# A Trainium2 kernel of attention and soft experts: small layer-norm and output steps given other places in the hand-written order of the expert stage

## The chip, the cores and the metric

The kernel runs on one core of one Trainium2 chip. The metric is the device time of one execution in microseconds (us), as the median of several runs. A profiled execution gives a trace of the core's engines: PE is TensorE's matrix multiply, PEld its weight load, DVE is VectorE, ACT is ScalarE, POOL is GpSimd, and SP is the engine that issues most transfers. Each engine works through its own queue strictly in order and waits on semaphores that the others raise.

## The reference, cut to what matters

The input x has 2 sequences of 1024 rows with 256 columns. An attention layer with 16 query heads and 4 key and value heads is added to x and layer-normed; a soft mixture of 16 experts with 128 slots each is added to that and layer-normed again. The change lies in the second half:

```python
x = _layernorm(x + attn(x, Wq, Wk, Wv, Wo, head_scale))
...
mean = jnp.mean(x, axis=-1, keepdims=True)
var = jnp.mean(jnp.square(x - mean), axis=-1, keepdims=True)
x_ln = (x - mean) / jnp.sqrt(var + LN_EPS) * gamma + beta
x_n = _l2norm(x_ln, -1) * scale
logits = jnp.einsum('bnd,des->bnes', x_n, _l2norm(mu, 0))
dispatch = softmax(logits, axis=1)
combine = softmax(logits.reshape(B, N, E * S), axis=-1)
slot_in = jnp.einsum('bnd,bnes->besd', x_ln, dispatch)
h = gelu(jnp.einsum('besd,edh->besh', slot_in, W1) + b1)
slot_out = jnp.einsum('besh,ehd->besd', h, W2) + b2
out = jnp.einsum('bsd,bns->bnd', slot_out, combine)
x = _layernorm(x + out)
```

All of it is float32; products are made of two or three passes over a high and a low part.

## The kernel before, in words

The program has two stages, attention for both sequences and then the experts (`experts`). Both are written as a plan: a Python list of steps in one order, from which every engine takes, in that order, the steps that are its own. So the plan fixes the order in each queue, and the semaphores do the rest. `plan_experts` (line 987) writes the list of the expert stage; the change touches only that function.

The expert stage goes through 32 pairs of sequence and expert, 16 of sequence 0 and then 16 of sequence 1. A **step** is one turn of the loop over `s` at line 1079, 35 in all: in step s the pair s is turned and dispatched, and the logits of pair s + 1 are made. Four pairs are a **unit** (u is the unit of the step, j the place within it); the unit before, v, is spread over the rows in the meantime. What a step has, with lines:

- PE turns `exps` of the pair in two halves (`turn`, L1488). ACT copies the first half into `dispatch` (`turned_a`, L1617) and DVE the second (`turned_b`, L1831); below they are the two **turned copies**.
- PE makes the next pair's logits (L1478). DVE takes their maximum (`top`, L1812), ACT the exponential (L1683) and a copy of the logits (`keep`, L1694), and DVE a running maximum (`run`, L1825) and an inverse of the sum (L1848).
- In steps with odd j PE widens two inverses (`wide_inverse`, L1498; it needs the PSUM bank that the first turned copy frees), and gathers (L1527; it needs both turned copies).
- With j = 3 PE turns the running maximum (`peaks`, L1546; it needs the bank that the second turned copy frees), DVE reduces it (`peak`, L1902), PE widens it (`wide`, L1555), and ACT and DVE copy that (`widened_a`, L1716, and `widened_b`, L1917). GpSimd then subtracts it from the four kept logits of the unit (L2006).
- With j = 1 and 2 the weights of unit v are taken apart into a high part on ACT (L1728) and a low part, three on GpSimd (L1986) and the fourth on DVE (`weight_lo_b`, L1895).
- With j = 2 the **spread** of unit v over the first four row tiles runs on PE (L1577), 12 matmuls a tile, and DVE adds each to `ffn_mixed` (`combine`, L1923 or L1927); the other four tiles follow with j = 0. The spread's tenth matmul of the first tile needs `weight_lo_b`.

Beside these stand the steps of two layer norms, which the change gives other places:

- Sequence 1's rows are normed while sequence 0's pairs run. `stats` is a `bn_stats` and a `bn_aggr` on DVE for each of 8 tiles (L1750, L1752), at the ends of steps 2 and 6, four tiles each. Then `deviations` (vary, std_1, inv_1, std_2, inv_2, offsets) alternates nine small DVE operations with two square roots on ACT (L1623). `centre` is four ACT passes over two tiles (L1639, L1644), `gamma` and `beta` two on GpSimd (L1996), and `squares` two on ACT (L1661); with tile pairs 0 and 1 of `centre` after step 7, pairs 2 and 3 and the first two `squares` after step 10, and the other two after step 11.
- Sequence 0's output is finished while sequence 1's pairs run. `finish` adds the expert output to a row tile on DVE (L1933) and `stats_3` takes its moments (L1750, L1752); three tiles at the end of step 18, three of step 22, two of step 26. `vary_3`, `std_3` (a square root on ACT, L1628, with its activation table), `inv_3` (three small DVE operations, L1957 to L1961), eight `normal_a` on ACT (L1632) and two stores follow in steps 26 to 30.

For sequence 1 the same end comes in the last spread, which runs tile by tile (L1570).

The finish of a row tile, as the engines take it:

```python
put(("finish", b, t), ("stats_3", b, t))
finish(0, {experts + 2: (0, 1, 2), experts + 6: (3, 4, 5), experts + 10: (6, 7)}.get(s, ()))
```

## Time and profile before

| | |
|---|---|
| median of 3 runs | 1204.24 us (1203.88 to 1205.72) |
| the profiled execution's own time | 1204.42 us |
| its span, first to last instruction | 1202.6 us |
| mean granted TensorE clock | 0.986 of full speed |
| PE busy | 1139.5 us (95%) |
| DVE, ACT, POOL busy | 804.0, 791.9, 712.2 us (67, 66, 59%) |
| expert stage | from about 838 us to the end |

The span is 1.8 us shorter than the execution's own time, since it leaves out what lies ahead of the first and behind the last instruction. A busy share is a mean over the program: it tells which engine is nearest to its limit, not which wait is worth something. That is read from the stretch itself: from the timeline, where a row gives in brackets how long its engine stood idle before it and what released it, and from the windows, which give busy time and granted clock of a stretch.

### The profile page before, as it was taken

To read this page: it belongs to the slowest core of one execution; us is meant where nothing else is said; L and a number is where in the kernel's file an instruction comes from. 1 tells how busy PE (TensorE), PEld (TensorE's weight loads), DVE (VectorE), ACT (ScalarE), POOL (GpSimd) and SP (SyncE) were. 2 spreads that over 40 slices of the span, in tenths; PEclk is the share of its full clock that TensorE was granted. 3 is DMA by queue.
4 is the path that set the end of the run, shared out by engine and by line. 5 is a ranking of instruction groups with operands and counts; after the bars stand their busy time and mean duration, and the time that the engine had idled before them with its cause. 6 is when DMAs were issued, how large, how long until landed. Compare 5 with 4: busy or idle time off the path is not lost. (4 is left out here: it accounts for less than half of the span.)

```text
span 1202.6 us, 23558 instructions
## 1 busy us (share of the span) xinstructions
PE 1139.5 (95%) x8096; PEld 1048.5 (87%) x8096; DVE 804.0 (67%) x1899; ACT 791.9 (66%) x1654; POOL 712.2 (59%) x485
## 2 busy tenths in 40 slices
PE   5899999999999999999999999999999999999977
PEld 4799999999998998899999999998778888898866
DVE  4575676666677568667676766776676575777767
ACT  2566766666675666678776766664477795567654
POOL 2677667667774765678676675530276654565521
PEclk9899999999999999999999999999999999999989
DMA  3231121111211112111111111200101101010011
GB/s 101 71 123 45 36 53 45 32 28 50 58 28 32 45 32 58 39 37 28 49 37 48 32 45 36 49 7 19 36 23 27 28 18 32 19 28 19 10 44 36
DMA packets 48789, 47.57 MB, mean 40 GB/s; under 512 B 13080, under 2 KB 43288, under 8 KB 48416
## 3 DMA queue, kind: packets, MB, share of 16 engines
q1 hardware_dynamic: 48384, 45.99, 14.8%
q8 instruction: 67, 1.10, 0.4%
q14 instruction: 50, 0.41, 0.1%
q10 hardware_dynamic: 288, 0.07, 0.0%
HBM read 24.03 MB, written 2.10 MB: 22 GB/s over the span
## 5 line engine op out<-in xcount | busy, mean ns | idle before, releaser
L536 PE MATMUL ring<-kT,qT 128*128 128x384 f32 (+5 forms) x1152 | 244.2, 347 | 3.1 <-ACT exps L701 2.6
L701 ACT ACTIVATE exps<-ring,neg_max 128x128 f32<-128x128 f32 (+7 forms) x256 | 189.3, 742 | 55.9 <-DVE neg_max L845 55.0
L845 DVE CUSTOM_DVE_ANT_0 ring<-ring,hidden 128x128 f32<-128x128 f32 (+7 forms) x256 | 191.6, 769 | 22.0 <-PE ring L536 21.1
L718 ACT ACTIVATE exp_parts<-turned 128x512 fp32r<-128x512 f32 x192 | 114.6, 597 | 133.9 <-PE turned L551 113.6
L536 PEld LDWEIGHTS ring<-kT,qT 128*128 128x128 f32 x1152 | 186.0, 189 | 14.3 <-issue 3.7
L572 PE MATMUL mix<-exp_parts,v_parts 128*128 128x256 f32 x1152 | 184.5, 296 | 0.4 <-DVE exp_parts L863 0.4
L551 PE MATMUL turned<-ident,exps 128*128 128x128 f32 x1152 | 178.5, 273 | 4.5 <-DVE exp_parts L863 3.8
L551 PEld LDWEIGHTS turned<-ident,exps 128*128 128x128 f32 x1152 | 141.3, 141 | 22.8 <-issue 3.6
L863 DVE TENSOR_TENSOR exp_parts<-turned,exp_parts 128x512 fp32r<-128x512 f32 x192 | 131.9, 687 | 29.3 <-ACT exp_parts L718 29.1
L572 PEld LDWEIGHTS mix<-exp_parts,v_parts 128*128 128x128 f32 x1152 | 149.4, 190 | 0.6 <-DVE exp_parts L863 0.6
L973 POOL TENSOR_TENSOR cos_part<-taken,cos_sb 128x1024 f32<-128x1024 f32 x38 | 91.3, 2402 | 94.7 <-ACT taken L669 94.7
L857 DVE TENSOR_TENSOR diag_parts<-turned,diag_parts 128x256 fp32r<-128x256 f32 x128 | 54.0, 422 | 123.4 <-ACT diag_parts L711 123.4
L510 PE MATMUL ring<-xT,parts 128*128 128x512 f32 x528 | 132.8, 401 | 2.2 <-ACT exps L701 2.2
L976 POOL TENSOR_TENSOR rotated<-rotated,sin_sb 128x1024 f32<-128x1024 f32 x38 | 91.1, 2398 | 71.1 <-DMA rotated<-taken 71.1
L510 PEld LDWEIGHTS ring<-xT,parts 128*128 128x128 f32 x528 | 97.1, 190 | 21.7 <-issue 2.6
L584 PE MATMUL ring<-wo_sb,mixed 128*128 128x256 f32 x768 | 105.9, 287 | 1.2 <-DVE mixed L851 1.2
L878 DVE SCALAR_TENSOR_TENSOR y_sb<-ring,inv_sum,y_sb 128x256 f32<-128x256 f32 x256 | 105.7, 476 | 0.4 <-PE ring L584 0.3
L584 PEld LDWEIGHTS ring<-wo_sb,mixed 128*128 128x128 f32 x768 | 96.3, 191 | 1.9 <-DVE mixed L851 1.8
L980 POOL TENSOR_TENSOR cos_part<-cos_part,rotated 128x1024 f32<-128x1024 f32 x38 | 91.2, 2401 | 5.4
L851 DVE TENSOR_TENSOR mixed<-mix,mixed 128x256 fp32r<-128x256 f32 x128 | 53.6, 419 | 60.3 <-ACT mixed L725 57.7
L1577 PE MATMUL ffn_spread<-ffn_slots,ffn_weights 128*128 128x258 f32 x672 | 87.3, 288 | 5.0 <-DVE ffn_weights L1895 4.8
L1577 PEld LDWEIGHTS ffn_spread<-ffn_slots,ffn_weights 128*128 128x128 f32 x672 | 84.9, 193 | 7.2 <-DVE ffn_weights L1895 5.9
(225 smaller groups left out, 2185.1 us busy)
## 6 DMA issues: line engine op xcount, KB each, us to landing
rotated<-taken SPq DMA_DIRECT2D x76, 256.0 KB, 3.7
raw_q<-in_L_attn_Wq_dram SPq DMA_DIRECT2D x32, 128.0 KB, 3.6
raw_o<-in_L_attn_Wo_dram SPq DMA_DIRECT2D x32, 128.0 KB, 3.3
ffn_mu_next<-in_L_ffn_mu_dram SPq DMA_DIRECT2D x28, 128.0 KB, 2.4
y_sb<-in_L_attn_x_dram SPq DMA_DIRECT2D x2, 1024.0 KB, 7.4
exps_and_mu<-in_L_ffn_mu_dram SPq DMA_DIRECT2D x1, 2048.0 KB, 9.6
ffn_w_sb<-in_L_ffn_W_dram SPq DMA_DIRECT2D x8, 256.0 KB
ffn_w_sb<-in_L_ffn_W_dram SPq DMA_DIRECT2D x14, 128.0 KB, 2.6
```

Of the source, the lines that this page charges most:

```text
L510: last = nc.tensor.matmul(ring_cols(item, half * BANK, BANK), w[:, a, c, :], xT[b][:, m, c, half * BANK:(half + 1) * BANK], start=k == 0, ...
L536: last = nc.tensor.matmul(ring_cols(item, half * BANK, piece), qT[:, H % QUERIES, a, i * P:(i + 1) * P], kT[:, G % 2, m, half * piece:(hal ...
L551: last = nc.tensor.transpose(bank[:, k * P:(k + 1) * P], exp_row(w, i)[:, j * P:(j + 1) * P], ident[:, :])
L572: last = nc.tensor.matmul(mix[:, window % 2, 0:PAIR], v_parts[:, G % 2, a, j * P:(j + 1) * P], parts[:, m, half * PAIR:(half + 1) * PAIR], ...
L584: last = nc.tensor.matmul(ring_cols(item, t * D, D), mixed[:, window % 2, a, t * P:(t + 1) * P], wo_sb[:, H % 2, m, :], start=k == 0, stop ...
L701: nc.scalar.activation(dst, tile, ACT.Exp, bias=neg_max[:, H % 2, i:i + 1], scale=-1.0, accum_out=row_sum[:, H % 2, i:i + 1]).then_inc(don ...
L718: nc.scalar.activation(exp_parts[:, slot % HELD, 0, :], turned[:, n % 2, :], ACT.Copy).then_inc(done[kind], 1)
L845: nc.vector.tensor_tensor_reduce(tile, tile, later, -1.0, 3.0e38, ALU.add, ALU.min, neg_max[:, H % 2, i:i + 1]).then_inc(done[kind], 1)
L863: nc.vector.tensor_tensor(exp_parts[:, slot % HELD, 1, :], turned[:, n % 2, :], exp_parts[:, slot % HELD, 0, :].bitcast(F32), ALU.subtract ...
L878: last = nc.vector.scalar_tensor_tensor(y_row, ring_cols(("output", H, w), t * D, D), inv_sum[:, H % 2, i:i + 1], y_row, ALU.mult, ALU.add)
L973: nc.gpsimd.tensor_tensor(part, taken[:, :], cos_sb[:, :], ALU.mult).then_inc(done[kind], 1)
L1577: last = nc.tensor.matmul(spread_ps[:, t % 2, 0:WIDE], weights[:, a, k, t * P:(t + 1) * P], slots[:, m, k, :], start=k == 0 and n == 0, st ...
```

## The change

Only the plan's order changes; no instruction is added or removed but one load of an activation table on ACT (the square root `std_3` of sequence 0 no longer stands between exponentials). PE's and SP's orders are the same as before.

- Sequence 1's `stats`: three tiles behind the turned copies of step 2 and one at its end, two behind the `peak` of step 3, two behind the turned copies of step 6. `vary` and `std_1` move up to just behind the exponential and `keep` of step 6; the rest of `deviations` stays at the end of the step, ahead of the parts of mu and W1.
- `centre` of pair 2 moves to the middle of step 10, behind the weight's high part; `centre` of pair 3 and the first `squares` into step 11 ahead of the peaks; the other three `squares` to the end of step 11.
- Sequence 0's `finish`: one tile at the end of steps 18 and 22 (two at the end of 26, as before), one behind the peak of steps 19 and 23, one behind the turned copies of steps 22 and 26.
- `std_3` of sequence 0 moves to the end of step 33, `inv_3`, the eight normals and the two stores into step 34, between the second and the third tile of the last spread.

```diff
--- before.py
+++ after.py
@@ -1001,7 +1001,7 @@
         put(*[("stats", b, t) for t in ts])
 
     def deviations(b):
-        put(*[(kind, b) for kind in ("vary", "std_1", "inv_1", "std_2", "inv_2", "offsets")])
+        put(*[(kind, b) for kind in ("inv_1", "std_2", "inv_2", "offsets")])
 
     def output(v):
         put(("output", v, 0), ("output", v, 1))
@@ -1054,18 +1054,32 @@
         put(*[("unit_hi", b, j) for j in js])
         put(*[("unit_lo", b, j) for j in js])
 
+    def centre(j):
+        put(("centre", 1, j), ("gamma", 1, j), ("beta", 1, j))
+
+    def beside_turn(s):
+
+        if sequences > 1:
+            moments(1, {2: (0, 1, 2), 6: (6, 7)}.get(s, ()))
+            finish(0, {experts + 6: (2,), experts + 10: (5,)}.get(s, ()))
+
+    def beside_peak(s):
+
+        if sequences > 1:
+            moments(1, {3: (4, 5)}.get(s, ()))
+            finish(0, {experts + 3: (1,), experts + 7: (4,)}.get(s, ()))
+
     def early(s):
 
         if sequences == 1:
             return
-        if s in (2, 6):
-            moments(1, range(s - 2, s + 2))
-        if s == 6:
-            deviations(1)
-        for j in {7: (0, 1), 10: (2, 3)}.get(s, ()):
-            put(("centre", 1, j), ("gamma", 1, j), ("beta", 1, j))
-        for j in {10: (0, 1), 11: (2, 3)}.get(s, ()):
-            put(("squares", 1, j))
+        if s == 2:
+            moments(1, (3,))
+        if s == 7:
+            centre(0)
+            centre(1)
+        if s == 11:
+            put(*[("squares", 1, j) for j in (1, 2, 3)])
         if s == 12:
             put(("inv_length", 1))
         if s == 13:
@@ -1092,6 +1106,7 @@
         if live:
             for half in range(2):
                 put(("turn", s, half), ("turned_b" if half else "turned_a", s, half))
+            beside_turn(s)
         if ripe and j == 1 and not last_unit:
             if not unfolded:
                 slots(v, 1)
@@ -1101,10 +1116,10 @@
             put(("weight", v, 3))
         if ripe and j == 2 and not last_unit:
             weight_parts(v, 3)
+            if s == 10 and sequences > 1:
+                centre(2)
         if ripe and j == 0 and not changed and not last_unit:
             put(("gelu", v))
-        if s == experts + 12 and sequences > 1:
-            put(("std_3", 0, 0))
         if s == experts - 4 and sequences > 1:
             put(("length", 1))
         if ahead and not change:
@@ -1119,6 +1134,9 @@
             slots(v, 1)
         if j == 3:
             split_mu(s + 3)
+        if s == 11 and sequences > 1:
+            centre(3)
+            put(("squares", 1, 0))
         if s == experts - 2 and sequences > 1:
             turn_units(1, (0, 1))
             put(("later_unit", 1, 2), ("later_unit", 1, 3))
@@ -1126,10 +1144,13 @@
             put(("peaks", u, 0), ("peaks", u, 1), ("peak", u, 0), ("peak", u, 1))
             if u % 4:
                 put(("fade", u), ("faded", u))
+            beside_peak(s)
         if ahead and not change:
             put(("exp", s + 1))
             if j != 3:
                 put(("keep", s + 1))
+        if s == 6 and sequences > 1:
+            put(("vary", 1), ("std_1", 1))
         if ripe and j == 0 and not last_unit:
             put(*[("weight", v, k) for k in (0, 1)])
         if ripe and j == 1 and not last_unit:
@@ -1168,6 +1189,10 @@
                 fold(1, 1)
         if j == 2:
             spread(v, (0, 1))
+        if s == total + 2 and sequences > 1:
+            put(("inv_3", 0, 0))
+            for half in range(2):
+                put(*[("normal_a", 0, 4 * half + t) for t in range(4)], ("store", 0, half))
         if j == 0 and not changed:
             spread(v - 1, (4, 5))
         if ahead and not change:
@@ -1189,6 +1214,8 @@
                 put(("output", v, 0))
                 if not unfolded:
                     put(("output", v, 1))
+        if s == 6 and sequences > 1:
+            deviations(1)
         if s + 4 < total:
             put((f"mu_load{s % 2}", s + 4))
         if j != 3:
@@ -1197,14 +1224,11 @@
             split_w1(u + 2)
         early(s)
         if sequences > 1:
-            finish(0, {experts + 2: (0, 1, 2), experts + 6: (3, 4, 5), experts + 10: (6, 7)}.get(s, ()))
+            finish(0, {experts + 2: (0,), experts + 6: (3,), experts + 10: (6, 7)}.get(s, ()))
             if s == experts + 10:
                 put(("vary_3", 0, 0))
-            if s == experts + 13:
-                put(("inv_3", 0, 0))
-            if s in (experts + 13, experts + 14):
-                half = s - experts - 13
-                put(*[("normal_a", 0, 4 * half + t) for t in range(4)], ("store", 0, half))
+            if s == total + 1:
+                put(("std_3", 0, 0))
     b = sequences - 1
     for part, ts in enumerate(((4, 5), (6, 7))):
         for t in ts:
```

Line numbers behind the diff's place are higher by 24 in the changed kernel (L1831 before is L1855 there).

**VectorE, end of step 6.** Before, the last of four tiles' moments, the deviations of sequence 1, and then the second turned copy of step 7 (the first row is the end of `stats`, the last is `turned_b`):

```order
L1752 BN_AGGR ffn_mean_var<-ffn_bn 128x2
L1766 TENSOR_SCALAR ffn_spread_sq<-ffn_mean_var 128x8
L1770 RECIPROCAL ffn_inv<-ffn_std 128x8
L1772 TENSOR_TENSOR ffn_inv<-ffn_inv 128x8
L1774 TENSOR_TENSOR ffn_inv<-ffn_inv,ffn_mean_var 128x8
L1776 TENSOR_SCALAR ffn_spread_sq<-ffn_inv 128x8
L1780 RECIPROCAL ffn_inv<-ffn_std 128x8
L1786 TENSOR_TENSOR ffn_inv<-ffn_inv 128x8
L1787 SCALAR_TENSOR_TENSOR ffn_offset<-ffn_mean_var,ffn_inv 128x8
L1789 TENSOR_TENSOR ffn_offset<-ffn_offset,ffn_inv 128x8
L1831 COPY ffn_dispatch<-ffn_turned 128x4x128
```

Now (L1836 and L1838 are `top` of pair 7, L1790 is `vary`, L1947 are the combines, L1849 and L1872 `run` and `inverse`):

```order
L1836 TENSOR_REDUCE ffn_neg_max<-ffn_ring 128x1
L1838 TENSOR_SCALAR ffn_neg_max<-ffn_neg_max,inv_mu 128x1
L1790 TENSOR_SCALAR ffn_spread_sq<-ffn_mean_var 128x8
L1947 COPY ffn_mixed<-ffn_spread 128x258 x2
L1849 TENSOR_TENSOR ffn_run<-ffn_run,exps_and_mu 128x1024
L1872 RECIPROCAL ffn_inv_total<-ffn_total 128x1
L1947 COPY ffn_mixed<-ffn_spread 128x258 x2
L1794 RECIPROCAL ffn_inv<-ffn_std 128x8
```

What moved: the moments are gone from the end of the step and `vary` stands ahead of the combines; the other eight small operations still stand between the last combine and the turned copy.

**ScalarE, steps 10 and 11.** Before, from the high part of the last weight in step 10 to the first turned copy of step 11 (L1639 and L1644 are `centre`, L1661 the `squares`, the last row but one is the copy):

```order
L1728 ACTIVATE ffn_weights<-exps_and_mu 128x1024
L1683 ACTIVATE ffn_exps,ffn_total<-ffn_ring,ffn_neg_max,inv_mu 128x1024
L1694 ACTIVATE ffn_kept<-ffn_ring,inv_mu 128x1024
L1591 ACTIVATE parts<-ffn_mu_next 128x256
L1600 ACTIVATE ffn_w_parts<-ffn_w_sb 128x512
L1639 ACTIVATE rows<-y_sb,ffn_offset,ffn_inv 128x256 x2
L1644 ACTIVATE y_sb<-y_sb,ffn_offset,ffn_inv 128x256 x2
L1639 ACTIVATE rows<-y_sb,ffn_offset,ffn_inv 128x256 x2
L1644 ACTIVATE y_sb<-y_sb,ffn_offset,ffn_inv 128x256 x2
L1661 ACTIVATE ffn_later,ffn_squared<-rows 128x256 x4
L1617 ACTIVATE ffn_dispatch<-ffn_turned 128x4x128
```

Now:

```order
L1752 ACTIVATE ffn_weights<-exps_and_mu 128x1024
L1663 ACTIVATE rows<-y_sb,ffn_offset,ffn_inv 128x256 x2
L1668 ACTIVATE y_sb<-y_sb,ffn_offset,ffn_inv 128x256 x2
L1707 ACTIVATE ffn_exps,ffn_total<-ffn_ring,ffn_neg_max,inv_mu 128x1024
L1718 ACTIVATE ffn_kept<-ffn_ring,inv_mu 128x1024
L1615 ACTIVATE parts<-ffn_mu_next 128x256
L1624 ACTIVATE ffn_w_parts<-ffn_w_sb 128x512
L1641 ACTIVATE ffn_dispatch<-ffn_turned 128x4x128
L1615 ACTIVATE ffn_mu<-ffn_mu_next 128x256
L1663 ACTIVATE rows<-y_sb,ffn_offset,ffn_inv 128x256 x2
L1668 ACTIVATE y_sb<-y_sb,ffn_offset,ffn_inv 128x256 x2
L1685 ACTIVATE ffn_later,ffn_squared<-rows 128x256 x2
```

What moved: one `centre` stands ahead of the exponential L1707, the other, with one of the four `squares`, behind the turned copy L1641; the copy follows the parts of mu and W1 directly.

**ScalarE, steps 29 to 31 and the end.** Before (L1632 are the normals, L1617 the turned copies, L1728 the high part of a weight):

```order
L1683 ACTIVATE ffn_exps,ffn_total<-ffn_ring,ffn_neg_max,inv_mu 128x1024
L1694 ACTIVATE exps_and_mu<-ffn_ring,inv_mu 128x1024
L1728 ACTIVATE ffn_weights<-ffn_kept 128x1024
L1632 ACTIVATE y_sb<-y_sb,ffn_offset,ffn_inv 128x256 x4
L1617 ACTIVATE ffn_dispatch<-ffn_turned 128x4x128
L1728 ACTIVATE ffn_weights<-ffn_kept 128x1024
L1683 ACTIVATE ffn_exps,ffn_total<-ffn_ring,ffn_neg_max,inv_mu 128x1024
L1694 ACTIVATE exps_and_mu<-ffn_ring,inv_mu 128x1024
L1632 ACTIVATE y_sb<-y_sb,ffn_offset,ffn_inv 128x256 x4
L1617 ACTIVATE ffn_dispatch<-ffn_turned 128x4x128
L1710 ACTIVATE ffn_fade<-ffn_fade 128x8
```

Now, the same place, and then the end of the program (L1656 are the normals, L1652 the square roots):

```order
L1718 ACTIVATE exps_and_mu<-ffn_ring,inv_mu 128x1024
L1752 ACTIVATE ffn_weights<-ffn_kept 128x1024
L1641 ACTIVATE ffn_dispatch<-ffn_turned 128x4x128
L1752 ACTIVATE ffn_weights<-ffn_kept 128x1024
L1707 ACTIVATE ffn_exps,ffn_total<-ffn_ring,ffn_neg_max,inv_mu 128x1024
```

```order
L1746 ACT_TABLE_LOAD
L1746 ACTIVATE exps_and_mu<-exps_and_mu 128x512 x8
L1652 ACT_TABLE_LOAD
L1652 ACTIVATE ffn_std<-ffn_spread_sq 128x8
L1656 ACTIVATE y_sb<-y_sb,ffn_offset,ffn_inv 128x256 x8
L1652 ACTIVATE ffn_std<-ffn_spread_sq 128x6
L1656 ACTIVATE y_sb<-y_sb,ffn_offset,ffn_inv 128x256 x6
L1652 ACTIVATE ffn_std<-ffn_spread_sq 128x2
```

What moved: both groups of four normals have left the steps 29 and 30, and all eight stand in the last spread behind a square root of their own.

## Rows read from the trace of the kernel before

**Rows 1.** Waits of TensorE from 838 us on: total, times, longest.

```profile
PE ffn_turned L1546 <- DVE ffn_dispatch L1831: 5.8, 6, 1.9
```

**Rows 2.** Windows: stretch, length, busy (count) by engine, granted clock, DMA share, GB/s.

```profile
907.20:913.50 6.30, 5.81 (x51) 5.13 (x51) 3.78 (x8) 3.11 (x6) 0.72 (x1) 0.73 0.01 3
913.50:926.00 12.50, 12.50 (x95) 11.88 (x94) 7.56 (x12) 12.08 (x22) 11.45 (x5) 1.00 0.00 1
...
952.70:958.30 5.60, 5.60 (x51) 4.86 (x51) 3.13 (x6) 1.69 (x5) 1.67 (x2) 0.70 0.08 23
...
1042.40:1046.50 4.10, 4.10 (x51) 3.76 (x52) 2.81 (x6) 1.84 (x4) 0.00 (x0) 1.00 0.01 4
...
1160.10:1168.00 7.90, 7.85 (x47) 7.61 (x47) 4.35 (x9) 4.82 (x8) 0.00 (x0) 0.71 0.15 51
```

**Rows 3.** Timeline of steps 2 and 3: start, us, engine, line, [idle before <- releaser].

```profile
860.53 1.23 DVE L1812 TENSOR_REDUCE ffn_neg_max<-ffn_ring 128x1 f32<-128x1024 f32 x1 [1.13 <-PE ffn_ring L1478]
...
865.74 0.41 DVE L1750 BATCH_NORM_STATS2 ffn_bn<-y_sb 128x6 f32<-128x256 f32 x1
...
867.86 0.67 DVE L1831 COPY ffn_dispatch<-ffn_turned 128x512 f32<-128x512 f32 x1
...
868.68 1.07 PE L1546 MATMUL ffn_turned<-ident,ffn_run 128*128 128x128 f32 x8 [0.83 <-DVE ffn_dispatch L1831]
```

**Rows 4.** Timeline of steps 6 and 7, VectorE and TensorE.

```profile
902.22 0.74 DVE L1923 COPY ffn_mixed<-ffn_spread 128x258 f32<-128x258 f32 x2
...
907.26 0.40 PE L1498 MATMUL ffn_turned<-ident,ffn_inv_total 128*128 128x128 f32 x2 [1.51 <-ACT ffn_dispatch L1617]
```

**Rows 5.** Timeline of steps 10 and 11, ScalarE and TensorE.

```profile
942.95 1.21 ACT L1683 ACTIVATE ffn_exps<-ffn_ring,ffn_neg_max,inv_mu 128x1024 f32<-128x1024 f32 x1 [2.68 <-DVE ffn_neg_max L1814]
...
947.24 1.09 ACT L1644 ACTIVATE y_sb<-y_sb,ffn_offset,ffn_inv 128x256 f32<-128x256 f32 x2
...
952.66 0.40 PE L1498 MATMUL ffn_turned<-ident,ffn_inv_total 128*128 128x128 f32 x2 [2.17 <-ACT ffn_dispatch L1617]
```

**Rows 6.** Timeline of steps 18 and 19, VectorE and TensorE.

```profile
1039.46 0.45 DVE L1933 SCALAR_TENSOR_TENSOR y_sb<-y_sb,ffn_mixed 128x256 f32<-128x256 f32 x1
...
1042.38 1.07 PE L1546 MATMUL ffn_turned<-ident,ffn_run 128*128 128x128 f32 x8 [1.90 <-DVE ffn_dispatch L1831]
...
1046.40 0.69 DVE L1917 COPY ffn_peak_wide<-ffn_turned 128x512 f32<-128x512 f32 x1 [1.26 <-PE ffn_turned L1555]
```

**Rows 7.** Timeline of steps 22 to 27, GpSimd, VectorE and TensorE.

```profile
1069.69 2.50 POOL L1986 TENSOR_TENSOR ffn_weights<-ffn_kept,ffn_weights 128x1024 fp32r<-128x1024 f32 x1 [2.35 <-ACT ffn_weights L1728]
...
1072.12 1.23 DVE L1895 TENSOR_TENSOR ffn_weights<-ffn_kept,ffn_weights 128x1024 fp32r<-128x1024 f32 x1 [1.20 <-ACT ffn_weights L1728]
...
1072.80 5.91 PE L1577 MATMUL ffn_spread<-ffn_slots,ffn_weights 128*128 128x258 f32 x48
...
1084.10 1.06 PE L1546 MATMUL ffn_turned<-ident,ffn_run 128*128 128x128 f32 x8 [1.56 <-DVE ffn_dispatch L1831]
...
1125.17 1.06 PE L1546 MATMUL ffn_turned<-ident,ffn_run 128*128 128x128 f32 x8 [0.90 <-DVE ffn_dispatch L1831]
```

**Rows 8.** Timeline of steps 29 and 30, all engines.

```profile
1152.54 2.49 POOL L1986 TENSOR_TENSOR ffn_weights<-ffn_kept,ffn_weights 128x1024 fp32r<-128x1024 f32 x1 [2.97 <-ACT ffn_weights L1728]
...
1152.98 2.07 DVE L1959 TENSOR_TENSOR ffn_inv<-ffn_inv 128x8 f32<-128x8 f32 x1
...
1155.29 2.07 ACT L1632 ACTIVATE y_sb<-y_sb,ffn_offset,ffn_inv 128x256 f32<-128x256 f32 x4 [2.83 <-DVE ffn_offset L1961]
...
1160.10 5.16 PE L1577 MATMUL ffn_spread<-ffn_slots,ffn_weights 128*128 128x258 f32 x24 [4.38 <-DVE ffn_weights L1895]
```

**Rows 9.** Timeline of the last spread, TensorE and VectorE.

```profile
1180.39 14.11 PE L1570 MATMUL ffn_spread<-ffn_slots_last,exps_and_mu 128*128 128x258 f32 x64
...
1193.84 0.19 DVE L1957 RECIPROCAL ffn_inv<-ffn_std 128x6 f32<-128x6 f32 x1 [0.27 <-ACT ffn_std L1628]
...
1194.38 0.48 DVE L1927 SCALAR_TENSOR_TENSOR ffn_mixed<-ffn_mixed,ffn_fade,ffn_spread 128x258 f32<-128x258 f32 x1
```

## The prediction

> **What bounds the kernel now.** I began with the waits of TensorE over the expert stage. TensorE is busy nearly all the time there, so time can come only from its gaps and from the stretches in which its clock is down. The largest group of gaps is `peaks` waiting for the second turned copy, on VectorE: 5.8 us in six waits [rows 1]. That copy is no work of its own; it is queued behind something else on VectorE. So the next view was the timeline ahead of each such gap, to see what is queued there [rows 3 to 8], and the last view the windows, to see what the gaps do to the clock [rows 2]. The windows show a second price: of the stretches right behind the gaps, three run at a mean granted clock of 0.73, 0.70 and 0.71 (a mix of 1.2 and 2.4 GHz), while the one behind the gap of step 19 stays at 1.00.
>
> In every one of these gaps the work in the way belongs to a layer norm that is due much later. The change moves just that work, so the question is how much of each gap goes, and what is late next.
>
> **The change part by part.** Times are counted from the profiled execution, 1204.42 us, which is 0.18 us above the median of 1204.24.
>
> *Steps 2 and 3.* Four tiles' moments stand from 865.74 to 867.86, 0.53 us each, ahead of the turned copy; `peaks` waits 0.83 us for it [rows 3]. Now three of them (1.6 us) stand ahead of `top`, where VectorE is idle for 1.13 us [rows 3]: `top`, and behind it the exponential and TensorE's next turn, come about 0.45 late, and the gap of 0.83 goes. Net -0.4 us; the bounds are -0.83 (the delay is hidden) and +0.45 (the gap stays). The two tiles in step 3 stand ahead of `widened_b`, for which VectorE idles longer than their 1.06 us: 1.26 in the row of the same place a sequence later [rows 6]. They cost nothing; were that cover gone, they would delay a copy that GpSimd waits for, by 1.06.
>
> *Steps 6 and 7.* Four tiles' moments and the deviations stand between the last combine (902.22 + 0.74 = 902.96) and the turned copies; `wide_inverse` waits 1.51 us, until 907.26 [rows 4]. Now the moments and `vary` are gone from there. Eight small operations and one square root remain, some 0.2 us each: done at about 904.8, before TensorE wants the copies (907.26 - 1.51 = 905.75). On ScalarE `std_2` now waits ahead of the parts of mu and W1, which are due steps later, and GpSimd's low parts follow them. So the wait goes: -1.5 at least. With it goes the fall of the clock, worth 6.30 x 0.27 = 1.7 us [rows 2]; together -3.2. But ScalarE is busy 12.08 of the next 12.50 us [rows 2], so it cannot come forward by more than its own small idle time, and TensorE will soon wait for it. I take -2.7, nearer to the upper bound, since the gap and most of the fall are surely gone.
>
> *Steps 10 and 11.* Four `centre` passes and two pairs of `squares` stand ahead of the first turned copy on ScalarE; TensorE waits 2.17 us [rows 5], and the window after it runs at 0.70, worth 5.60 x 0.30 = 1.7 [rows 2]. Now the first `centre` of these (two groups of two passes at 1.09, 2.2 us) stands ahead of an exponential for which ScalarE idles 2.68 us [rows 5], and so is hidden. The second, with one `squares`, stands in the stretch where ScalarE is busy 1.69 of 5.60 us [rows 2]. GpSimd's `gamma` and `beta` follow their `centre` and are due only for the `squares`. Bounds -2.2 and -3.9; what ScalarE then does is as in the step before, with one pair of `squares` more behind it. I take -2.8.
>
> *Steps 18 and 19.* Three tiles' finishes stand ahead of the turned copy, each 0.45 us and 0.53 of moments, about 1.0; `peaks` waits 1.90 [rows 6]. Now one stays: VectorE is 2.0 earlier, the whole wait goes, -1.9. The tile that moves behind the `peak` stands ahead of `widened_b`, where VectorE idles 1.26 [rows 6]: free.
>
> *Steps 22 and 23, 26 and 27.* In both a finish now stands ahead of `weight_lo_b`, where VectorE idles 1.20 us [rows 7], seemingly room for 1.0. But at that time GpSimd is busy with a pass of 2.50 us that ends at 1072.19, just when `weight_lo_b` starts at 1072.12 [rows 7]. In step 29 a VectorE operation on 8 elements, begun at 1152.98 beside such a pass, ended at 1155.05, with the pass (1152.54 + 2.49 = 1155.03) [rows 8]: an operation on two SBUF tensors waits until GpSimd is through. A finish is such an operation. It would start at about 1072.2, and with its moments push `weight_lo_b` back by 1.1 us (bounds: 0, if it is not held up, and 1.6, if GpSimd's next pass gets in between as well). The spread feels about half of it at once (its tenth matmul is due at 1072.80 + 9/48 of 5.91 = 1073.9, `weight_lo_b` is done at 1073.35 [rows 7]), and VectorE's own queue all of it. In step 22 two finishes leave the end of the step: 2.0 - 1.1 = 0.9 of the wait of 1.56 [rows 7] goes, -0.9 (bounds -1.56 and -0.4). In step 26 nothing leaves the end, and `peaks`, which already waits 0.90 for VectorE [rows 7], comes 1.1 later: +1.1 (bounds 0 and +1.6). The finish behind the `peak` of step 23 is hidden as in step 19.
>
> The Trainium skill, Advanced Engine Details and Errata, Mode Summary, has GpSimd and VectorE block each other only where VectorE runs a mode that reads one tensor through both ports; read so, a finish, with two input tensors, would not be held up. GPSIMD Engine Reference, Specifications, adds instructions with two SBUF inputs, and the row of step 29 agrees with that page. By the first page alone the sum would be 1.8 us lower.
>
> *Steps 29 to 31.* `inv_3` (held up by GpSimd as above), four normals (2.07 us, after 2.83 of idle ScalarE) and only then the weight's high part: the spread waits 4.38 us for `weight_lo_b`, until 1160.10 [rows 8], and then runs 7.90 us at 0.71, 2.3 of them lost [rows 2]. Now ScalarE goes straight on. `weight_lo_b` is then held by GpSimd's pass until 1155.03 and done 1.23 later, 1156.26, while TensorE wants it at 1160.10 - 4.38 = 1155.72: a wait of 0.5 remains. So -(4.38 + 2.3 - 0.5) = -6.2; if the clock falls all the same, -3.8. I take -5.9, near the upper end, as the rest of the step resembles step 26. The second four normals stood where ScalarE waits anyway: nothing. The table load that disappears is on ScalarE ahead of an exponential that TensorE does not wait for: nothing.
>
> *The last spread.* `inv_3` costs VectorE 1194.38 - 1193.84 = 0.54 us [rows 9] between the second and third tile. TensorE needs 14.11/8 = 1.76 us a tile [rows 9], and VectorE about 1.5 (combine 0.48, finish 0.45, moments 0.53), so VectorE wins it back over four tiles. The normals fall on an idle ScalarE, the stores on an idle queue, ahead of sequence 1's. I take +0.1 of 0 to +0.54.
>
> Sum: -0.4 - 2.7 - 2.8 - 1.9 - 0.9 + 1.1 - 5.9 + 0.1 = -13.4 us. 1204.42 - 13.4 = 1191.0, and 0.18 less for the median: **1190.8 us**.
>
> **The rivals.**
>
> *The clock stays as low as before.* If new small waits keep it falling (ends at 1.5, 2.2 and 3.8 in steps 7, 11 and 30), the sum is -9.5: 1194.7. For it: two of three falls followed gaps no longer than that of step 19. Against it: that one, of 1.90, had no fall behind it. The Trainium skill, TensorE: Matmul & The Clock Gate, What's actually happening, lets the recent busyness set the clock; by it falls leave with their gaps, as three of the four stretches bear out. Chance 0.15.
>
> *A finish beside GpSimd is not held up.* Then step 22 gains its whole 1.56 and step 26 loses nothing: 1.8 less, 1189.0. The operation of step 29 speaks against it. Chance 0.10; the first of the two pages above says this.
>
> *The change does not free step 30.* If `weight_lo_b` is late for another reason than the normals, 5.9 stays: 1196.7. Against it: ScalarE's idle 2.83 us names `inv_3` [rows 8]. Chance 0.05.
>
> *Slower.* The new waits in the spreads (steps 6, 22 and 26: two tiles' moments in the first, a finish in the others, all ahead of `weight_lo_b`) drop the clock, and each spread of 5.91 us [rows 7] runs at half speed: 3 x (5.9 + 0.6) = 19.5 against 13.4, +6.1 us, 1210.3. It decides once all three fall. Against it: 1.90 us of waiting dropped nothing, and these are of 0.6. Chance 0.03.
>
> **How the numbers follow.** The forecast has 0.63, and 0.04 is left for several misses together, close to no change. A measurement of this kernel tells 0.2% (2.4 us) from no change. Faster by more: 0.63 + 0.15 + 0.10 + 0.05 = 0.93; same 0.04; slower 0.03. The range takes in all favourable bounds (-17.6, 1186.6) and the first rival with some 2 us of further misses: 1186.0 to 1196.5.
>
> **What would show it.** TensorE waits for no copy at `wide_inverse` of steps 7 and 11; `peaks` of step 19 follows at once; the windows behind steps 7, 11 and 30 show a clock of 1.00; step 30's spread waits about half a microsecond. The finishes of steps 22 and 26 last 1 to 1.7 us instead of 0.45, and `peaks` of step 27 waits about 2 us. The prediction is wrong if TensorE waits just as long elsewhere: for the exponentials, or for turned copies queued behind ScalarE's backlog.

## The result and the profile after

The changed kernel takes 1190.18 us in the median of 4 runs (1189.51 to 1191.42), the kernel before 1204.06 (1203.38 to 1205.72, 4 runs) beside it: ratio 0.9887, 95% interval 0.9874 to 0.9901. The forecast was 1190.8 with a range of 1186.0 to 1196.5. The profiled execution of the changed kernel took 1189.53 us, against 1204.42 before. Lines behind the diff have moved by 24: L1488 is now L1512.

The waits of TensorE over the expert stage (total, times, longest), where [rows 1] had 5.8 us in six waits for the second turned copy at `peaks`:

```profile
PE ffn_turned L1512 <- ACT ffn_exps L1707: 5.7, 5, 1.6
PE ffn_spread L1601 <- DVE ffn_weights L1919: 1.4, 5, 0.4
PE ffn_small L1551 <- DVE ffn_dispatch L1855: 1.3, 2, 0.7
PE ffn_turned L1570 <- DVE ffn_dispatch L1855: 1.1, 2, 0.9
...
PE ffn_turned L1522 <- ACT ffn_dispatch L1641: 0.6, 2, 0.3
```

At `peaks` (L1570) one wait for that copy is left that counts, the 0.90 of step 27, and the waits for the first turned copy at `wide_inverse` (L1522) have shrunk from 4.3 us in four to 0.6 in two. The exponentials, with 5.7 us in five waits, are now the largest group; they were 5.5 in four before. The spread (L1601) waits 1.4 us for `weight_lo_b` in five waits, at most 0.45 at a time; before it was 4.8 in three, with 4.38 of it in step 30. The gathers (L1551) wait 1.3 us for the second turned copy, where it was 0.6.

The windows behind the places of [rows 2] (stretch, length, busy by engine, granted clock, DMA share, GB/s):

```profile
904.87:912.29 7.42, 7.32 (x76) 6.56 (x75) 4.42 (x10) 5.05 (x9) 3.23 (x3) 1.00 0.23 55
...
946.33:953.74 7.41, 7.24 (x75) 6.58 (x74) 4.31 (x9) 4.58 (x13) 3.33 (x3) 1.00 0.20 54
...
1033.01:1040.42 7.41, 7.24 (x75) 6.56 (x74) 5.18 (x12) 3.74 (x6) 2.02 (x1) 1.00 0.18 45
...
1063.98:1070.30 6.32, 6.02 (x50) 5.81 (x49) 4.49 (x8) 3.24 (x5) 0.88 (x2) 1.00 0.07 21
...
1145.53:1152.00 6.47, 6.02 (x49) 5.81 (x48) 4.79 (x6) 2.42 (x3) 0.54 (x1) 1.00 0.01 3
```

These are, in order, behind the gaps of steps 7, 11 and 19, and the spreads of steps 22 and 30. All run at 1.00, which is 2.4 GHz throughout; a lower mean is a mix with 1.2 GHz. Before, the stretches behind steps 7, 11 and 30 ran at 0.73, 0.70 and 0.71 [rows 2].

The timeline of the changed kernel at the places of [rows 3 to 8]:

```profile
863.34 1.09 PE L1512 MATMUL ffn_turned<-ident,ffn_exps 128*128 128x128 f32 x8 [0.40 <-ACT ffn_exps L1707]
...
904.87 0.38 PE L1522 MATMUL ffn_turned<-ident,ffn_inv_total 128*128 128x128 f32 x2
...
946.33 0.38 PE L1522 MATMUL ffn_turned<-ident,ffn_inv_total 128*128 128x128 f32 x2
...
1033.22 0.61 PE L1570 MATMUL ffn_turned<-ident,ffn_run 128*128 128x128 f32 x4
...
1060.88 2.50 POOL L2010 TENSOR_TENSOR ffn_weights<-ffn_kept,ffn_weights 128x1024 fp32r<-128x1024 f32 x1 [2.35 <-ACT ffn_weights L1752]
...
1062.02 1.64 DVE L1957 SCALAR_TENSOR_TENSOR y_sb<-y_sb,ffn_mixed 128x256 f32<-128x256 f32 x1
...
1065.51 4.95 PE L1601 MATMUL ffn_spread<-ffn_slots,ffn_weights 128*128 128x258 f32 x39 [0.30 <-DVE ffn_weights L1919]
...
1103.04 1.64 DVE L1957 SCALAR_TENSOR_TENSOR y_sb<-y_sb,ffn_mixed 128x256 f32<-128x256 f32 x1
...
1106.52 4.95 PE L1601 MATMUL ffn_spread<-ffn_slots,ffn_weights 128*128 128x258 f32 x39 [0.30 <-DVE ffn_weights L1919]
...
1110.37 1.23 DVE L1849 TENSOR_TENSOR ffn_run<-ffn_run,ffn_kept 128x1024 f32<-128x1024 f32 x1 [1.26 <-ACT ffn_kept L1718]
...
1116.22 1.06 PE L1570 MATMUL ffn_turned<-ident,ffn_run 128*128 128x128 f32 x8 [0.90 <-DVE ffn_dispatch L1855]
...
1144.96 2.19 DVE L1919 TENSOR_TENSOR ffn_weights<-ffn_kept,ffn_weights 128x1024 fp32r<-128x1024 f32 x1 [0.36 <-ACT ffn_weights L1752]
...
1147.21 4.96 PE L1601 MATMUL ffn_spread<-ffn_slots,ffn_weights 128*128 128x258 f32 x39 [0.45 <-DVE ffn_weights L1919]
```

What to see there. Step 3's first turn (863.34) now waits 0.40 for its exponential. `wide_inverse` of step 7 (904.87) and of step 11 (946.33) and `peaks` of step 19 (1033.22) begin with no wait beside them, where there stood 1.51, 2.17 and 1.90 [rows 4 to 6]. The finishes of steps 22 and 26 (1062.02, 1103.04) last 1.64 us each and end 0.28 after GpSimd's pass (1060.88 + 2.50 = 1063.38); both spreads then wait 0.30 for the weight's low part. In step 30 that low part (1144.96) lasts 2.19 beside GpSimd's pass, and the spread waits 0.45 instead of 4.38 [rows 8].

A sharper measure than the medians is where each step begins, by TensorE's first turn in it. This is the difference between the two traces, after minus before, gathered by place; the first column, ahead, is the difference that is there already at the start of the expert stage, in front of every edit. The column 6-11 has what the steps 6 to 10 gave, and so on:

| kernel | ahead | steps 0-6 | 6-11 | 11-18 | 18-22 | 22-23 | 23-24 | 24-27 | 27-28 | 28-31 | tail | stage, 0-31 |
|---|---|---|---|---|---|---|---|---|---|---|---|---|
| changed kernel | -0.41 | -0.28 | -3.32 | -3.08 | -1.73 | +0.58 | -1.36 | +0.64 | 0.00 | -5.96 | +0.02 | -14.51 |

### The profile page after: what moved, and what is told of

Read it like the earlier page. It is cut to its first block and busy times, and to the rows that moved or that the text cites. A ratio compares the mean times of both kernels' runs of the same rounds, so it can differ in the third digit from the quotient of the medians.

```text
span 1187.7 us, 23557 instructions
## 1 busy us (share of the span) xinstructions
PE 1135.0 (96%) x8096; PEld 1043.9 (88%) x8096; DVE 805.2 (68%) x1899; ACT 790.4 (67%) x1653; POOL 709.8 (60%) x485
## 5 line engine op out<-in xcount | busy, mean ns | idle before, releaser
L1601 PE MATMUL ffn_spread<-ffn_slots,ffn_weights 128*128 128x258 f32 x672 | 86.1, 284 | 1.6 <-DVE ffn_weights L1919 1.4
L1601 PEld LDWEIGHTS ffn_spread<-ffn_slots,ffn_weights 128*128 128x128 f32 x672 | 83.2, 189 | 4.3 <-DVE ffn_weights L1919 3.0
```

What stands on the lines that cost most here:

```text
L1601: last = nc.tensor.matmul(spread_ps[:, t % 2, 0:WIDE], weights[:, a, k, t * P:(t + 1) * P], slots[:, m, k, :], start=k == 0 and n == 0, st ...
```

## Experiments: which part does what

The first three put one part of the change alone into the kernel before.

**Sequence 0's norms late** (`std_3` to step 33, `inv_3`, the normals and their stores to step 34):

```diff
-        if s == experts + 12 and sequences > 1:
-            put(("std_3", 0, 0))
...
+        if s == total + 2 and sequences > 1:
+            put(("inv_3", 0, 0))
+            for half in range(2):
+                put(*[("normal_a", 0, 4 * half + t) for t in range(4)], ("store", 0, half))
...
-            if s == experts + 13:
-                put(("inv_3", 0, 0))
-            if s in (experts + 13, experts + 14):
-                half = s - experts - 13
-                put(*[("normal_a", 0, 4 * half + t) for t in range(4)], ("store", 0, half))
+            if s == total + 1:
+                put(("std_3", 0, 0))
```

> The kernel before with one part of the change alone: sequence 0's std_3, inv_3, normals and stores moved from steps 28 to 30 into steps 33 and 34. Theory (the normals stood ahead of the weight's high part on ScalarE, and the gap of 4.38 us dropped the clock): step 30's spread waits about 0.45 us, its window runs at a clock of 1.00, the last step's first turn comes 5.9 us earlier, the tail takes as long as before; profiled time 1198.5 us. Rival 1 (the clock falls there for another reason): 3.8 us, 1200.6. Rival 2 (the gain needs the other two parts): less than 3 us.

**Sequence 1's statistics alone** (`moments`, `deviations`, `centre`, `squares` as in the changed kernel, the rest as before):

```diff
+            moments(1, {2: (0, 1, 2), 6: (6, 7)}.get(s, ()))
...
+            moments(1, {3: (4, 5)}.get(s, ()))
...
-        if s in (2, 6):
-            moments(1, range(s - 2, s + 2))
-        if s == 6:
-            deviations(1)
...
```

> The kernel before with the moves of sequence 1's statistics alone (moments, deviations, centre, squares; steps 2 to 12). Theory: as in the changed kernel, -0.3 us by step 4, -3.3 by step 10, -3.1 more by step 14, in all -6.7: profiled time 1197.7. No window behind steps 7 and 11 shows a clock under 1.00. Rival (part of these gains came from what else the change moved): smaller sums at the same steps, or the clock down in one of the two windows (1.7 us back for each, 1199.4 or 1201.1).

**Sequence 0's finishes alone:**

```diff
+            if sequences > 1:
+                finish(0, {experts + 6: (2,), experts + 10: (5,)}.get(s, ()))
...
+            if sequences > 1:
+                finish(0, {experts + 3: (1,), experts + 7: (4,)}.get(s, ()))
...
-            finish(0, {experts + 2: (0, 1, 2), experts + 6: (3, 4, 5), experts + 10: (6, 7)}.get(s, ()))
+            finish(0, {experts + 2: (0,), experts + 6: (3,), experts + 10: (6, 7)}.get(s, ()))
```

> The kernel before with the spreading of sequence 0's finishes alone (steps 18 to 27). Theory: -1.7 us at step 19, +0.6 in the spread of step 22 and -1.4 at step 23, +0.6 in the spread of step 26; in all -1.9 us, profiled time 1202.5. The finishes of steps 22 and 26 last 1.64 us each. If the three parts add up, e1, e2 and e3 together make -14.5 us, against the -14.9 of the whole change; a rival, that the parts help one another, has a sum smaller by 1 us or more.

| kernel (one execution each) | time | ahead | 0-6 | 6-11 | 11-18 | 18-22 | 22-23 | 23-24 | 24-27 | 27-28 | 28-31 | tail | stage |
|---|---|---|---|---|---|---|---|---|---|---|---|---|---|
| norms late | 1198.13 | -0.27 | -0.01 | +0.03 | -0.02 | 0.00 | +0.01 | +0.01 | -0.01 | 0.00 | -6.02 | -0.02 | -6.01 |
| statistics | 1201.58 | +2.38 | -0.24 | -3.41 | -3.09 | +1.62 | 0.00 | 0.00 | 0.00 | -0.01 | -0.10 | +0.05 | -5.23 |
| finishes | 1200.54 | -1.19 | +0.01 | +0.01 | -0.03 | -1.73 | +0.57 | -1.35 | +0.56 | 0.00 | -0.73 | +0.08 | -2.69 |

Every part does at its own places what it does in the whole change, to within 0.1 us: the parts do not need one another. The norms alone hit the expected 1198.5 within 0.4. The other two missed by some 4 and 2 us, and not through their edits. Most of that is the first column, the attention stage, which no edit touches and which ended 2.38 us later in the one execution and 1.19 earlier in the other. What is left stands in two cells where the edit does nothing: +1.62 in the steps 18 to 22 of the one, -0.73 in the steps 28 to 31 of the other. The rows of both (timeline and window, first of the statistics alone, then of the finishes alone):

```profile
1038.03 1.15 PE L1569 MATMUL ffn_turned<-ident,ffn_run 128*128 128x128 f32 x8 [1.91 <-DVE ffn_dispatch L1854]
...
1038.03:1042.10 4.07, 4.07 (x36) 3.82 (x38) 2.72 (x5) 1.30 (x2) 0.00 (x0) 0.60 0.01 4
```

```profile
1156.92 6.28 PE L1581 MATMUL ffn_spread<-ffn_slots,ffn_weights 128*128 128x258 f32 x39 [4.38 <-DVE ffn_weights L1899]
...
1156.90:1164.80 7.90, 7.53 (x49) 7.10 (x49) 4.96 (x9) 4.97 (x8) 0.00 (x0) 0.81 0.15 50
```

In the first, the gap of step 19 is as long as before, 1.91 against 1.90 [rows 6], but this time the clock fell behind it, to 0.60, where it had stayed at 1.00 [rows 2]. In the second, the gap of step 30 is the same 4.38, but the clock came back sooner, a mean of 0.81 against 0.71. So whether the gap of 1.9 us drops the clock, and for how long the longer one does, differs between executions of the same steps. Without those two cells the three parts make -6.01 - 6.85 - 1.96 = -14.8, against -14.5 for the whole.

**The norms behind the high part of the weight, not out of the way** (kernel before; `inv_3` and the first four normals, which stood at the end of step 29, go into step 30, the other four stay at its end):

```diff
             weight_parts(v, 3)
+            if s == experts + 14:
+                put(("inv_3", 0, 0), *[("normal_a", 0, t) for t in range(4)], ("store", 0, 0))
...
-            if s == experts + 13:
-                put(("inv_3", 0, 0))
-            if s in (experts + 13, experts + 14):
-                half = s - experts - 13
-                put(*[("normal_a", 0, 4 * half + t) for t in range(4)], ("store", 0, half))
+            if s == experts + 14:
+                put(*[("normal_a", 0, 4 + t) for t in range(4)], ("store", 0, 1))
```

> The kernel before with sequence 0's inv_3 and first four normals behind the high part of the weight in step 30 instead of ahead of it (the other four stay at the end of that step). Theory (what cost 5.9 us is that they stood ahead of that high part, not their work): step 30's spread waits 0.45 us as in the changed kernel, the clock stays at 1.00, the exponential of step 31 starts up to 1.2 us later but ends before the spread does; profiled time 1198.5 us, 5.5 to 5.9 below the kernel before. Rival (ScalarE has no room for 2.07 us of normals in these steps at all): the exponential comes too late for step 31's turn, 2 us are given back, 1200.5 or more.

It took 1200.06 us. The steps 28 to 31 gave -5.50, as the theory says; but 0.86 came back in step 31. The timeline of TensorE and ScalarE:

```profile
1156.43 2.06 PE L1576 MATMUL ffn_spread<-ffn_slots,ffn_weights 128*128 128x258 f32 x15 [0.46 <-DVE ffn_weights L1894]
...
1158.72 3.14 PE L1576 MATMUL ffn_spread<-ffn_slots,ffn_weights 128*128 128x258 f32 x24 [0.24 <-DVE ffn_mixed L1926]
...
1161.23 2.06 ACT L1631 ACTIVATE y_sb<-y_sb,ffn_offset,ffn_inv 128x256 f32<-128x256 f32 x4
...
1163.92 0.40 PE L1497 MATMUL ffn_turned<-ident,ffn_inv_total 128*128 128x128 f32 x2 [1.18 <-ACT ffn_dispatch L1616]
```

The wait for the weight is 0.46, so the place in ScalarE's order was what cost 4.38 us and the clock, not the work. The work does show twice. `inv_3` now delays `combine`, for which the spread waits 0.24. And the second four normals (1161.23) hold up the first turned copy of step 31, for which TensorE waits 1.18. They cost nothing in the same place before, but there the spread ran some 6 us later and the copy was wanted later with it; here, too, the first four delay the exponential and all that follows it on ScalarE. So the rival was right in part: ScalarE does not have room for all eight in these two steps once the spread is on time. How many have room was not tried; in the changed kernel, which moves both halves out, TensorE waits 0.3 there.

## Experiments: what a gap does to the clock

The kernel before, with its own moments and finishes shared out otherwise, so that gaps grow or shrink:

```diff
-            moments(1, range(s - 2, s + 2))
+            moments(1, {2: range(5), 6: range(5, 8)}[s])
...
-            finish(0, {experts + 2: (0, 1, 2), experts + 6: (3, 4, 5), experts + 10: (6, 7)}.get(s, ()))
+            finish(0, {experts + 2: (0, 1, 2, 3), experts + 6: (4, 5, 6, 7)}.get(s, ()))
```

> The kernel before with its own work shifted between steps, so that the gaps of TensorE change in length: five moments at the end of step 2 and three at the end of step 6 (four and four before); four finishes each at the end of steps 18 and 22, none in step 26 (three, three and two before). Gaps by the durations before: 1.4 us in step 3, 1.0 in step 7 (with the 0.43 behind it), 2.2 in step 11, 2.9 in step 19, 2.6 in step 23, none in step 27. Theory (the length of a gap decides over the clock: those up to 1.6 us drop none, 1.9 us is the edge, those over 2 us do): no fall behind step 7, falls behind steps 11, 19 and 23. Step changes against the kernel before: +0.5, -2.2, 0, +2.7, +2.7, -0.9; profiled time 1207.2 us. Rival (the place decides, not the length: the step that fell falls, the one that did not does not): step 7 gains 0.5, steps 19 and 23 lose 1.0 each; 1205.5.

It took 1208.03 us (0.46 of it from the attention stage), and the changes by step were +0.5, -2.1, +0.3, +2.4, +2.5 and -0.7, all near the theory and far from the rival in steps 7, 19 and 23. Timeline and windows:

```profile
907.70 0.40 PE L1498 MATMUL ffn_turned<-ident,ffn_inv_total 128*128 128x128 f32 x2 [0.99 <-ACT ffn_dispatch L1617]
...
1042.67 1.94 PE L1546 MATMUL ffn_turned<-ident,ffn_run 128*128 128x128 f32 x8 [2.97 <-DVE ffn_dispatch L1831]
...
1086.80 1.94 PE L1546 MATMUL ffn_turned<-ident,ffn_run 128*128 128x128 f32 x8 [2.61 <-DVE ffn_dispatch L1831]
...
907.00:912.60 5.60, 4.48 (x53) 3.96 (x54) 4.31 (x12) 3.21 (x6) 0.72 (x1) 1.00 0.17 43
...
1042.67:1046.70 4.03, 4.03 (x38) 3.70 (x40) 2.72 (x5) 1.29 (x2) 0.00 (x0) 0.64 0.02 4
...
1086.80:1090.80 4.00, 4.00 (x36) 3.67 (x38) 2.89 (x6) 1.01 (x2) 0.00 (x0) 0.61 0.00 0
```

The gap of step 7, 0.5 us shorter, no longer drops the clock (1.00; it was 0.73 [rows 2]); those of steps 19 and 23, lengthened by 1.0, now do (0.64 and 0.61). One more gap, which no edit touches, belongs beside these: in step 5 TensorE waits 1.56 us for an exponential. The timeline and the window behind it, in the kernel before and then in the statistics alone:

```profile
880.56 1.23 PE L1488 MATMUL ffn_turned<-ident,ffn_exps 128*128 128x128 f32 x8 [1.56 <-ACT ffn_exps L1683]
...
887.02 1.97 PE L1527 MATMUL ffn_small<-ffn_dispatch,ffn_folded 128*64 128x128 f32 x32 [0.61 <-DVE ffn_dispatch L1831]
...
880.56:886.46 5.90, 5.84 (x22) 4.35 (x22) 4.74 (x5) 5.90 (x8) 5.83 (x4) 0.71 0.26 63
```

```profile
882.65 1.09 PE L1511 MATMUL ffn_turned<-ident,ffn_exps 128*128 128x128 f32 x8 [1.57 <-ACT ffn_exps L1706]
...
889.15 1.97 PE L1550 MATMUL ffn_small<-ffn_dispatch,ffn_folded 128*64 128x128 f32 x32 [1.53 <-DVE ffn_dispatch L1854]
...
882.65:888.55 5.90, 4.49 (x22) 3.21 (x22) 4.74 (x5) 5.90 (x8) 5.87 (x4) 1.00 0.28 64
```

The clock falls there to a mean of 0.71 in the one and stays at 1.00 in the other. Put together over the executions of all kernels that have the gap:

| gap of TensorE | executions in which the clock fell behind it |
|---|---|
| 0.99, and 0.43 right behind (step 7, gaps changed) | 0 of 1 |
| 1.33 (step 2, waiting for an exponential) | 0 of 13 |
| 1.56 (step 5, waiting for an exponential) | 12 of 13 |
| 1.56 (step 23) | 0 of 4 |
| 1.90 (step 19) | 1 of 4 |
| 1.51, and 0.43 right behind (step 7) | 4 of 4 |
| 2.17 (step 11) | 5 of 5 |
| 2.61 and 2.97 (steps 23 and 19, gaps changed) | 2 of 2 |
| 4.38 (step 30) | 4 of 4 |

So the theory that the length of the gap decides fits the edited steps but not step 5: of two gaps of the same 1.56 us, one nearly always dropped the clock and the other never did. What TensorE did before them differs: ahead of the gap in step 5 stand eight matmuls that use 65 of the 128 rows (L1537), ahead of that in step 23 only full ones. Whether that is the reason was not tried.

The second of the waits in step 7, which stands right behind the first, in the kernel before:

```profile
908.09 1.39 PE L1546 MATMUL ffn_turned<-ident,ffn_run 128*128 128x128 f32 x8 [0.43 <-DVE ffn_dispatch L1831]
```

A fall cost 1.5 to 1.6 us behind the gaps of steps 7, 11 and 19 (3.56 - 1.94, 3.65 - 2.17, and the +1.62 above), and 0.7 less in one of the executions of step 30 than in the others. In step 5 it cost nothing: without the fall TensorE waits 1.53 us instead of 0.61 for the next turned copy and begins its gathers just as late, 6.50 us behind the step's first turn against 6.46. The Trainium skill, TensorE: Matmul & The Clock Gate, What's actually happening, has a monitor of recent activity that runs on freely whatever the program does; a gap of 1.9 us that drops the clock in one execution and not in the next agrees with that.

## Experiments: the finish beside GpSimd, and a version that beats both

The changed kernel, with the finishes of steps 22 and 26 behind the second combine of the same step:

```diff
-            finish(0, {experts + 6: (2,), experts + 10: (5,)}.get(s, ()))
...
             spread(v, (0, 1))
+            if sequences > 1:
+                finish(0, {experts + 6: (2,), experts + 10: (5,)}.get(s, ()))
```

> The changed kernel with the two finishes that stand beside GpSimd's pass (steps 22 and 26) put behind the second combine of the same step, where VectorE idles 1.34 and 1.26 us and GpSimd is idle. Theory (a finish is held up by GpSimd's pass, nothing else is wrong with it): each lasts 0.48 instead of 1.64 us, the waits of 0.30 us for the weight's low part go in both spreads, each step 0.57 us shorter, the 0.90 us ahead of step 27's peaks stay: profiled time 1189.53 - 1.14 = 1188.4. Rival (VectorE has too much to do in these steps wherever the finish stands): the run, the exponential's keep or the turned copies come later by up to 1 us, and the time is 1189.5 or more.

It took 1188.33 us, against an expected 1188.4: steps 22-23 at 0.00 instead of +0.58, steps 24-27 at +0.07 instead of +0.64, all else as in the changed kernel. Timeline of step 22, and the `peaks` of step 27:

```profile
1063.93 5.91 PE L1602 MATMUL ffn_spread<-ffn_slots,ffn_weights 128*128 128x258 f32 x48
...
1067.36 0.48 DVE L1958 SCALAR_TENSOR_TENSOR y_sb<-y_sb,ffn_mixed 128x256 f32<-128x256 f32 x1
...
1115.02 1.06 PE L1571 MATMUL ffn_turned<-ident,ffn_run 128*128 128x128 f32 x8 [0.90 <-DVE ffn_dispatch L1856]
```

The same finish lasts 0.48, and the spread runs through in 5.91. Going on from there, all eight finishes were put where VectorE idles and GpSimd does too, and `vary_3` behind the peaks of step 31:

```diff
-            finish(0, {experts + 6: (2,), experts + 10: (5,)}.get(s, ()))
...
-            finish(0, {experts + 3: (1,), experts + 7: (4,)}.get(s, ()))
+            finish(0, {experts + 3: (1,), experts + 7: (3,), experts + 11: (6,)}.get(s, ()))
+            if s == total - 1:
+                put(("vary_3", 0, 0))
...
             spread(v, (0, 1))
+            if sequences > 1:
+                finish(0, {experts + 2: (0,), experts + 6: (2,), experts + 10: (4,), experts + 14: (7,)}.get(s, ()))
...
-            finish(0, {experts + 2: (0,), experts + 6: (3,), experts + 10: (6, 7)}.get(s, ()))
-            if s == experts + 10:
-                put(("vary_3", 0, 0))
+            finish(0, {experts + 10: (5,)}.get(s, ()))
```

> The changed kernel with all of sequence 0's finishes at places where VectorE idles and GpSimd has nothing: tiles 0, 2, 4, 7 behind the second combine of steps 18, 22, 26, 30, tiles 1, 3, 6 behind the peaks of steps 19, 23, 27, tile 5 at the end of step 26; vary_3 behind the peaks of step 31, where VectorE idles 0.90 us. Theory: the 0.57 us in each of steps 22 and 26 and the 0.90 ahead of step 27's peaks go, every finish lasts about 0.5 us: profiled 1187.5, 2.0 below the changed kernel, median 1188.1 against 1190.2. Rival (the places are full once they are used: run, widened_b or gathered come later and TensorE waits there): no gain over the changed kernel, 1189.5 to 1190.2.

> The changed kernel unaltered, beside the kernel before and the version of the run before this one on the same chip. Theory: 14 us below the kernel before, ratio 0.988, 2 us above the version with all finishes at free places. Rival: that version and this one cannot be told apart.

> The version with all finishes at free places once more, unaltered, beside the changed kernel on one chip. Theory: its expert stage is 2.0 us shorter than the changed kernel's in the profile, its median 1 to 2 us lower. Rival: the stage before the experts varies by more than that between executions, so that the medians lie within 1 us of each other.

> The changed kernel unaltered, as the other side of that comparison: median 1189 to 1190, its expert stage by steps within 0.1 us of its earlier two profiles.

The eight finishes of sequence 0 as one group (count, total, mean ns), in the changed kernel and then in this version:

```profile
L1957 DVE SCALAR_TENSOR_TENSOR y_sb<-y_sb,ffn_mixed 128x256 f32<-128x256 f32 x8 | 8.1, 1011 | 0.0
```

```profile
L1958 DVE SCALAR_TENSOR_TENSOR y_sb<-y_sb,ffn_mixed 128x256 f32<-128x256 f32 x8 | 3.8, 478 | 0.0
```

| kernel | median | ratio to the kernel before, 95% interval | stage, 0-31, by trace |
|---|---|---|---|
| changed, second and third time | 1188.72, 1189.78 | 0.9876 (0.9861 to 0.9891), 0.9879 (0.9862 to 0.9895) | -14.55, -14.76 |
| finishes at free places, twice | 1187.74, 1187.74 | 0.9864 (0.9848 to 0.9881), 0.9861 (0.9845 to 0.9877) | -16.49, -16.48 |
| statistics moved too (below) | 1186.32 | 0.9853 (0.9838 to 0.9868) | -17.95 |

By the traces the version gains 1.7 to 2.0 us over the changed kernel, where 2.0 was expected, and its own stage comes out the same twice: the 0.57 of steps 22 and 26 each goes, and 0.70 of the 0.90 ahead of step 27's `peaks` (0.17 is left, for `inverse_wide`). By the medians it is 1 and 2 us ahead, with intervals that overlap; the profiled executions of this version alone began the expert stage 4.3 us apart (+1.30 and -3.01), which is the rival's point: what is gained is shown by the traces, not by the medians.

Last, three items of sequence 1's statistics, to see whether what the change gives back behind its gains is the queue's doing (cut to the new places):

```diff
...
+        if s == 7 and sequences > 1:
+            put(("centre", 1, 0))
         if s == 11 and sequences > 1:
             centre(3)
-            put(("squares", 1, 0))
+            put(*[("squares", 1, j) for j in (0, 1, 2)])
...
+        if s == 1 and sequences > 1:
+            moments(1, (0, 1, 2))
...
```

> The version with all finishes at free places, and three items of sequence 1's statistics moved once more: the three moments of step 2 ahead of the run of step 2, one step earlier, where VectorE idles 1.82 us; the first centre of step 7 ahead of the fade, where ScalarE idles 2.37 us; two of the three pairs of squares of the end of step 11 ahead of its fade, where ScalarE idles 2.83 us. Theory (what the changed kernel gives back behind its gains is ScalarE's and VectorE's queue: +0.37 at step 3, +0.10 and +0.16 at steps 9 and 10, +0.14 and +0.42 at steps 13 and 14): the 0.37 goes, of the 0.26 and 0.56 about half; the expert stage is 0.8 us shorter, median 1187.0. Rival (they are the price of the shift ahead of them, GpSimd and the folds, not of the queue): nothing changes but step 3.

The stage came out 1.46 us shorter still, where 0.8 was expected: step 3's 0.37 went, some 0.2 of the 0.26 behind step 7, 0.43 of the 0.56 behind step 11, and 0.43 more in step 10, whose spread had waited in the kernel before as well:

```profile
933.93 6.28 PE L1606 MATMUL ffn_spread<-ffn_slots,ffn_weights 128*128 128x258 f32 x48
```

Its 48 matmuls run without a break, where the changed kernel's wait 0.19 after the ninth: ScalarE starts on the weight's last high part 1.86 us behind the step's first turn, where it was 2.67. So the time went and came back with the places in the queues, VectorE's in step 3 and ScalarE's in the others, as the theory has it; the three moves were made together and are told apart only by where they act. Against the kernel before this version saves 1.47% and is the best of the study; against the changed kernel the intervals just overlap, and the traces put it 3.2 to 3.4 us ahead.

## Why the prediction was right

By its own steps, in the trace:

| step of the prediction | forecast | measured |
|---|---|---|
| 2 and 3 | -0.4 | -0.3 (+0.37, then -0.66) |
| 6 and 7 | -2.7 | -3.3 (-3.56, then +0.26 back) |
| 10 and 11 | -2.8 | -3.1 (-3.65, then +0.56 back) |
| 18 and 19 | -1.9 | -1.7 (0.17 is left, for `inverse_wide`) |
| 22 and 23 | -0.9 | -0.8 (+0.58, -1.36) |
| 26 and 27 | +1.1 | +0.6 |
| 29 to 31 | -5.9 | -6.0 |
| last spread | +0.1 | 0.0 |
| sum | -13.4 | -14.5 |

*The gaps and their falls.* The two prices of a gap, its length and the clock behind it, were both there. Step 7 gave 3.56 where the forecast had 1.51 + 1.7 = 3.2: the wait of 0.43 right behind, which the forecast left out, went as well. Step 11 gave 3.65 of 2.17 + 1.7 = 3.9. The term that was mis-sized is what ScalarE takes back, put at 0.5 and some 1.1 us: it took 0.26 and 0.56. Steps 7 and 11 thus make 0.9 of the 1.1 us by which the sum fell short, and the next item 0.5; step 19 fell 0.2 short of its forecast, and small differences make up the rest.

*Steps 26 and 27.* The finish was held up, the spread lost 0.57; the step that failed is "VectorE's own queue all of it", by which step 27's `peaks` would wait 2 us. It waits 0.90 as before. VectorE idles 1.26 us ahead of `run` in the changed kernel (1110.37), and step 27's turn is itself 0.57 later, so nothing of the hold-up reaches the turned copy. A queue that idles between the delay and the place at risk, and for longer than the delay, does not hand it on.

*Step 30.* Within 0.1 us, with a remaining wait of 0.45 for a forecast 0.5; the order in ScalarE's queue was the cause, as the norms placed behind the high part show. (Without the gain of the clock the prediction's own numbers give 3.9, not 3.8.)

*The rivals.* "The clock stays as low" is out for this change, since all five windows are at 1.00; the one fall that stays, in step 5, is there before and after. But the argument against it, that a gap of 1.90 had no fall behind it, was luck: it falls in one execution of four. And the argument for it was misread: of the gaps 1.51, 2.17 and 4.38 only one, not two, is no longer than that of step 19. "A finish beside GpSimd is not held up" is out: 1.64 against 0.48; of the two pages of the Trainium skill that the prediction set against each other, GPSIMD Engine Reference, Specifications, is the one that the runs bear out. The note of the other names the modes with two read ports and does not say that nothing else is blocked; that "only" was the prediction's reading of it. "The change doesn't free step 30" is out. The slower rival, by which the three spreads drop the clock, is out: they wait 0.20 to 0.30, and the window of step 22's is at 1.00.

## What to carry to other kernels

In an in-order queue, small work that is due much later costs nothing where the engine idles. It costs its full length, and sometimes a fall of the clock on top, where it stands ahead of something that TensorE waits for: look for what is queued ahead of the late operation, not at the operation.

Whether a wait that is removed pays a second time, through the clock, could not be read from its length alone here. The gaps of 2.17 and 4.38 us always dropped the clock and one of 1.90 did in one execution of four; of two gaps of 1.56 one never did, and the other nearly always, at no cost, since TensorE had to wait right behind it anyway. So compare traces place by place from a common start, and more than one execution of each. Before filling an idle spot of VectorE, look at what GpSimd does just then.
